# First attention of a two-layer decoder: the relation's sums move from VectorE to GpSimd, its exponentials follow each other on ScalarE, and its logarithm and reciprocal stand two heads earlier

## The reference

```python
attn_scores = einsum('bihd,bjhd->bhij', q, k) / scale
li = x @ rel_W[:, :d].T
lj = x @ rel_W[:, d:].T
logits = li[:, :, None, :] + lj[:, None, :, :] + rel_b     # three relations
relation_probs = softmax(logits, axis=-1)
bias = einsum('bijk,hk->bhij', relation_probs, logical_bias)
gate = sigmoid(x @ gate_W.T + gate_b)
attn_scores = attn_scores + gate * bias
out = einsum('bhij,bjhd->bihd', softmax(attn_scores), v)
```

## Time and profile before

| | us |
|---|---|
| median of 3 executions | 6552.33 (6550.13 to 6559.78) |
| the profiled execution | 6533.35 |
| its span | 6531.6 |
| the stage's steady part, 170 to 1550 us of the span | 1380 |
| DVE busy over the whole span | 4018.2 (62%) |
| ACT busy | 3197.3 (49%) |
| POOL busy | 2323.1 (36%) |

### The profile page before, as it was taken

One profiled execution on the slowest core, in us unless ns is written; L12 is line 12 of the kernel. 1 busy time (PEld: TensorE's weight loads), 2 busy tenths in 40 slices (PEclk: granted clock), 3 DMA queues, 4 the chain that ended last, 5 costly groups with the idle time before them and its releaser, 6 DMA issues. The chain is left out here.

```text
span 6531.6 us, 143828 instructions
## 1 busy us (share of the span) xinstructions
PE 5530.0 (85%) x53632; PEld 3266.4 (50%) x53632; DVE 4018.2 (62%) x7302; ACT 3197.3 (49%) x4813; POOL 2323.1 (36%) x1900
## 2 busy tenths in 40 slices
PE   7788888887977996998897888778798999799998
PEld 3455555555854445777775555453222222344444
DVE  5999999997976554444443444356777777233333
ACT  5899999996556552222222333243355555211111
POOL 1887877885654333444442111143100000000000
PEclk8999999999989997999998999897899999899999
DMA  6111020201112333333332111144322221200000
GB/s 171 28 30 36 22 41 15 44 12 40 47 51 75 151 145 120 106 106 103 106 103 70 39 39 39 34 102 131 84 36 39 39 37 28 63 19 19 19 19 11
DMA packets 416489, 395.37 MB, mean 61 GB/s; under 512 B 232034, under 2 KB 370648, under 8 KB 407760
## 3 DMA queue, kind: packets, MB, share of 16 engines
q1 hardware_dynamic: 402128, 362.74, 20.0%
q10 hardware_dynamic: 13824, 25.17, 1.1%
HBM read 247.57 MB, written 140.23 MB: 59 GB/s over the span
## 5 line engine op out<-in xcount | busy, mean ns | idle before, releaser
L538 POOL TENSOR_SCALAR attn_u<-attn_rel,attn_aux 128x1024 f32<-128x1024 f32 x512 | 1089.1, 2127 | 270.7 <-DVE attn_nm L565 269.4
L689 PE MATMUL attn_tp<-attn_ident,attn_pr 128*128 128x128 f32 x4096 | 573.2, 284 | 241.5 <-ACT attn_pt L628 239.3
L3186 DVE TENSOR_REDUCE attn_mx<-attn_mp 128x1 f32<-128x512 f32 x1024 | 639.6, 682 | 195.7 <-PE attn_mp L3275 193.5
L3257 ACT ACTIVATE attn_pt<-attn_st 128x1024 f32<-128x1024 f32 x512 | 509.1, 1022 | 409.0 <-PE attn_st L3285 408.5
L557 DVE SCALAR_TENSOR_TENSOR attn_u<-attn_rel,attn_aux,attn_u 128x1024 f32<-128x1024 f32 x512 | 681.2, 1331 | 29.5 <-POOL attn_u L538 21.0
L689 PEld LDWEIGHTS attn_tp<-attn_ident,attn_pr 128*128 128x128 f32 x4096 | 449.7, 143 | 462.4 <-ACT attn_pt L628 323.1
L565 DVE CUSTOM_DVE_ANT_0 attn_pr<-attn_u,attn_s 128x1024 f32<-128x1024 f32 x512 | 618.4, 1208 | 45.5 <-PE attn_s L680 32.5
L649 ACT ACTIVATE attn_pr<-attn_pr,attn_nm 128x1024 f32<-128x1024 f32 x512 | 602.9, 1177 | 88.3 <-DVE attn_nm L565 88.1
L628 ACT ACTIVATE attn_pt<-attn_tp 128x512 f32<-128x512 f32 x1024 | 566.0, 621 | 11.1 <-PE attn_tp L689 5.6
L3275 PE MATMUL attn_mp<-attn_kt,attn_qt 96*128 96x512 bf16 x1024 | 371.9, 396 | 97.3 <-DVE attn_mx L3186 56.2
L3655 PE MATMUL moe_ps<-moe_w,moe_hidt 128*128 128x512 f32 x1024 | 453.2, 593 | 0.0
(11 more groups left out here) (492 smaller groups left out, 10548.8 us busy)
## 6 DMA issues: line engine op xcount, KB each, us to landing
s_qkv<-gin_qkv SPq DMA_DIRECT2D x32, 1536.0 KB, 5.1
core_qk<-s_qkv SPq DMA_DIRECT2D x32, 1024.0 KB, 5.1
attn_qt<-s_q SPq DMA_DIRECT2D x384, 64.0 KB, 2.9
attn_kt<-s_k SPq DMA_DIRECT2D x192, 128.0 KB, 4.3
core_arow<-s_alr SPq DMA_DIRECT2D x32, 512.0 KB, 3.8
core_grow<-s_gar SPq DMA_DIRECT2D x32, 512.0 KB, 3.7
...
```

The source lines that it names most:

```text
L538: pool.tensor_scalar(u[:, x % 4], rel[:, z % 2, 1], aux[:, s, 4 + NH + h:5 + NH + h], aux[:, s, 4 + 2 * NH + h:5 + 2 * NH + h], ALU.mult, ...
L689: ins = pe.transpose(tp[k][:, n], pr[:, x % BUF, (4 * k + n) * P:(4 * k + n + 1) * P], ident[:])
L3186: dve.reduce_max(mx[w % 2][:].rearrange("p h t a -> p (h t a)")[:, j:j + 1], mp[j % 2][:], AX.X).then_inc(m["max_done"], 1)
L3257: act.activation(pt[:, x % 4, 2 * a:2 * a + 2], st[a][:], ACT.Exp).then_inc(m["exp_done"], 1)
```

## The change

`relation_sum` is taken out of VectorE's stream and put into GpSimd's, with the same operation and the same semaphores: two sums ahead of the stream for the first tile, and for each later tile one after the u of head 6 and one after the u of head 9. On ScalarE the four exponentials stand after the exps of heads 0, 1, 2 and 3, the logarithm after that of head 7, the reciprocal after that of head 8, and the output of the tile before is taken out of PSUM after head 6 in place of 7. No buffer changes its size, and no other stage is touched.

```diff
--- before.py
+++ after.py
@@ -526,6 +526,12 @@
                 pool.tensor_copy(v32[:, :, at, 0:HD], vs[:, :, g * GR * HD:(g + 1) * GR * HD].rearrange("p n (h e) -> p n h e", e=HD)
                                  ).then_inc(m["v_ready"], 1)
 
+            def relation_sum(v, z, c):
+                pool.wait_ge(m["ex_done"], tile(v, z) * 2 + c + 1)
+                pool.tensor_tensor(rel[:, z % 2, c], ex[:, 2 * c], ex[:, 2 * c + 1], ALU.add).then_inc(m["sum_done"], 1)
+
+            for c in range(2):
+                relation_sum(0, 0, c)
             for v, k, b in bodies(pool):
                 for x in range(STREAM):
                     z, h = x // NH, x % NH
@@ -537,6 +543,8 @@
                     s = slot_of(k, z)
                     pool.tensor_scalar(u[:, x % 4], rel[:, z % 2, 1], aux[:, s, 4 + NH + h:5 + NH + h],
                                        aux[:, s, 4 + 2 * NH + h:5 + 2 * NH + h], ALU.mult, ALU.add).then_inc(m["u_done"], 1)
+                    if h in (6, 9) and not final(v, z):
+                        relation_sum(v, z + 1, (h - 6) // 3)
             for z in range(2):
                 pool.wait_ge(m[f"out{z}"], BODIES * 16)
 
@@ -544,10 +552,6 @@
         def _(dve):
             dve.sem_inc(m["ns_done"], 4)
             dve.sem_inc(m["row_done"], 1)
-
-            def relation_sum(v, z, c):
-                dve.wait_ge(m["ex_done"], tile(v, z) * 2 + c + 1)
-                dve.tensor_tensor(rel[:, z % 2, c], ex[:, 2 * c], ex[:, 2 * c + 1], ALU.add).then_inc(m["sum_done"], 1)
 
             def mix(v, k, x):
                 z, h = x // NH, x % NH
@@ -565,8 +569,6 @@
                 dve.tensor_tensor_reduce(pr[:, x % BUF], u[:, x % 4], sc[x % 2][:].rearrange("p a n -> p (a n)"), -1.0, 3e38,
                                          ALU.add, ALU.min, nm[:, x // NH % 2, x % NH:x % NH + 1]).then_inc(m["ns_done"], 1)
                 z, h = x // NH, x % NH
-                if h in (5, 9) and not final(v, z):
-                    relation_sum(v, z + 1, (h - 5) // 4)
                 if h == NH - 1:
                     dve.wait_ge(m["ns_done"], tile(v, z + 1) * NH + 4)
                     dve.sem_inc(m["q_free"], 1)
@@ -583,8 +585,6 @@
                                   rs[:].rearrange("p (h o) -> p h o", o=1).to_broadcast([P, NH, HD]), ALU.mult).then_inc(m["row_done"], 1)
                 link.done()
 
-            for c in range(2):
-                relation_sum(0, 0, c)
             for v, k, b in bodies(dve):
                 for x in range(STREAM):
                     mix(v, k, x)
@@ -648,13 +648,13 @@
                     act.wait_ge(m["ns_done"], head(v, x) + 5)
                     act.activation(pr[:, x % BUF], pr[:, x % BUF], ACT.Exp, bias=nm[:, z % 2, h:h + 1], scale=-1.0).then_inc(m["exp_done"], 1)
                     if not final(v, z):
-                        if h in (0, 2, 4, 6):
-                            relation(v, k, z + 1, b + 1 if k == PER - 1 and z == NT - 1 else None, h // 2)
-                        if h == 9:
+                        if h < 4:
+                            relation(v, k, z + 1, b + 1 if k == PER - 1 and z == NT - 1 else None, h)
+                        if h == 7:
                             relation_log(v, z + 1)
-                        if h == 10:
+                        if h == 8:
                             relation_end(v, z + 1)
-                    if h == 7 and begun(v, (z - 1) * NH):
+                    if h == 6 and begun(v, (z - 1) * NH):
                         evacuate(v, z - 1)
                     if h == 15 and begun(v, (z - 1) * NH):
                         store(v, z - 1)
```

## The result

The changed kernel takes 6683.41 us (median of 4 runs, 6676.05 to 6696.85) against 6551.23 (4 runs, 6549.64 to 6559.78) of the one before: a ratio of 1.0201, 95% interval 1.0182 to 1.0221. It is 132 us slower. The forecast was 6627, or 74 us slower, with a range up to 6672: the sign is right, the size is not, and the time lies outside the range. The profiled execution took 6696.85 us, with a span of 6695.0.

The account below looks back on a forecast made before the run. VectorE and ScalarE were both taken as full, neither alone setting the time, with the VectorE-GpSimd port as full as VectorE. -2.28 + 4.06 + 0.62 = +2.40 us a tile, x 31 = +74: 6627 us, range 6572 to 6672.

Parts of the forecast that it names:

- VectorE's sums go: First attention, VectorE's stream: two sums of 1.14 us leave each of 31 tiles, -2.28 us a tile.
- The sums hold mixes 5 and 8: GpSimd's sums, behind the u's of heads 6 and 9, block VectorE's mixes 5 and 8 by 2.03 us each: +4.06 a tile.
- the row with 2048 columns: GpSimd two-operand instruction of 4515 ns; half of it gave the forecast's sum length, 2.26 us for 1024 columns.
- the row of 1024 columns with the repeated operand: GpSimd instruction of 1.91 us, basis of the short-sum rival: +53 us, 6605, or 6586; chance 0.15.
- Mixes of about 3.3: Sign to look for: two mixes a tile, heads 5 and 8, of about 3.3 us in place of 1.27.
- Who wins the port: At mixes 5 and 8 the GpSimd sum, shown first, gets the shared SBUF port and blocks VectorE's mix.
- the rival: Mix 5 wins the port, the sum holds mix 6: 0.23 us more each, +14 us, 6641; within the forecast's 0.56.
- Four exponentials in a row: ScalarE's lag reaches 2.8 us at exp 4, which would hold score 6 by 1.7; mix 5's hold covers it: 0.
- The late wait: Logarithm and reciprocal in adjacent heads make score 11 late by 1.83 us, in place of 1.21 before: +0.62 a tile.
- The lag: How much later a ScalarE exp starts than right behind its score; forecast 2.90 us at exp 9.
- longer waits for TensorE: Rival: longer gaps ahead of the transposes of heads 8 and 9 add +29 (6656) to +58 us (6685); chance 0.14.
- Or if another stage changes: Stated sign that the whole prediction is wrong: a stage other than the first attention changes; no size given.

Follow-up runs that it names:

- those of 1168.37 and 1168.79: Rows of the kernel before with only the two sums moved to GpSimd, ScalarE's order kept: 6617.06 us, ratio 1.0116.
- sums of 64 columns: The changed kernel, but GpSimd adds only 64 of the 1024 columns in each sum: 6600.29 us, ratio 1.0088.
- the gaps filled: The changed kernel with TensorE making the products of heads 2 and 9 four times over, in its gaps: 6672.43 us, ratio 1.0190.
- The fillers: One-column VectorE memsets in the changed kernel where its sums stood: 6649.99 us; one-column GpSimd additions in the kernel before where the change puts sums: 6542.01 us.

## Why the prediction was wrong in its size

**VectorE's sums go: right.** -2.28 us a tile; none is left in the stream.

**The sums hold mixes 5 and 8: right in place and mechanism, a little short.** Forecast 2.03 us each and +4.06; measured 2.03 and 2.06 by head beyond the 1.27, 2.12 each if all that the mixes gained (131.7 us) is put on the 62 sums. The sum takes 2.36 us instead of 2.26: half of the row with 2048 columns was the nearest, the row of 1024 columns with the repeated operand was not. The two terms together came to 131.7 - 70.7 = +61 us where the forecast had 31 x 1.78 = 55. "Mixes of about 3.3" is 3.42 in the rows.

**Who wins the port: right, and the rival was priced wrongly.** All 62 sums of the changed kernel held their mix, as the rows of 1179.37 and 1179.39 show; those of 1168.37 and 1168.79 show a mix that came first and kept its length. The Trainium skill, SBUF — State Buffer, section "Who interferes with whom", says that the order of issue decides who blocks, and these rows agree. The starts shown don't settle it to 0.02 us, though: 59 of those sums are shown 0.01 to 0.03 us ahead of the mix and all held it, while 21 u's of the same profile, as close ahead of a mix as the one in the earlier trace rows, all lost to it. What set the two cases apart no run here tested; the sums stand straight behind a u, those u's behind a wait. In the price, "the whole 2.26 would come out" was wrong: a lost race cost 1.82 in the tile shown, where part of the sum lies beside a score.

**Four exponentials in a row are covered by the hold: right.** No wait at heads 4 to 6 after; with sums of 64 columns 1.06 us of the 1.7 showed there.

**The late wait: the step that failed in the changed stage.** The forecast had 1.83 at score 11 in place of 1.21, +0.62 a tile, 19 us. Measured: 2.91 at heads 10 and 11 in place of 1.25, and 53.6 us more idle time ahead of the scores. The lag was counted rightly: exp 9 starts 2.93 us late (the median over the tiles) where the forecast had 2.90, and with the gaps filled the waits are 2.03 us a tile against its 1.83. What was missing is that the hold empties ScalarE, that the logarithm follows at once, and that TensorE after the 2.86 us gap so made works at a granted clock of 0.50. The forecast kept the durations of TensorE as they were at 1.00. Of the 35 us that this term lacked, some 27 went with the filled gaps (99.1 - 71.6). The rival "longer waits for TensorE" had the mechanism's outcome, and at +29 to +58 us its numbers hold the 35 us that were missing; its 0.14 was too low. That the measured 6683 lies where it does in that rival's band owes 25 us to another stage: with the terms of the changed stage alone it would be 6627 + 6 + 35 = 6668. The trace of before had the reason ready: in the tile whose wait was 3.01 us, TensorE's window just before that score shows a granted clock of 0.65, where it is 1.00 from 676 to 680 and again behind 687:

```profile
683.00:687.00 4.00, 4.00 (x39) 2.68 (x41) 0.99 (x2) 3.33 (x5) 1.82 (x1) 0.65 0.00 0
```

The prediction used the wait as a bound and did not ask for the clock behind it.

**"Or if another stage changes": it did, and the sum had no term for it.** It is 25 us in the second attention, a cost that the diff doesn't show and no row of before could size. The fillers show that it comes from what was taken out of VectorE's stream; by what mechanism stays open. It took both missing pieces to put the time above the range's upper end of 6672: without this one it would be 6683 - 25 = 6658, without the missing part of the late wait 6683 - 35 = 6648.

By the terms: 74 forecast, +6 for the sum's length (61 for 55), +35 for the late wait (53.6 for 19), +25 for the second attention: 140, against 132 by the medians.
